# A head's outputs copied behind two exponentials of the next head, and added behind the second low part

## What is computed

```python
# attention: 32 query heads, 8 key/value heads of 64, rope, causal mask
attn = jnp.einsum('bkgqd,bkld->bkgql', qh, kh) * SCALE
attn = jnp.where(causal[None, None, None], attn, -jnp.inf)
p = jax.nn.softmax(attn, axis=-1)
out = jnp.einsum('bkgql,bkld->bkgqd', p, vh)
...
return out @ Wo.T
...
x = _layernorm(x + attn_ref(x, Wq, Wk, Wv, Wo))
x = _layernorm(x + xattn_ref(x, fside, ctx))      # two SmoothQuant int8 products with silu between
x = _layernorm(x + ffn_ref(x, up, down, scales))  # sign weights, relu, 512 -> 2048 -> 512
```

## Time and profile before

| | |
|---|---|
| median of 3 runs | 1396.93 us (1396.26 to 1397.88) |
| the profiled execution | 1396.48 us, its span 1394.7 us |
| PE busy (matmuls) | 1295.6 us, 93% of the span |
| DVE busy | 1011.3 us, 73% |
| ACT busy | 905.3 us, 65% |
| POOL busy | 782.9 us, 56% |
| granted TensorE clock | 0.98 of full speed |

### The profile page before, as it was taken

One profiled execution on the slowest core, in us unless ns is written; L12 is line 12 of the kernel. 1 busy time (PEld: TensorE's weight loads), 2 busy tenths in 40 slices (PEclk: granted clock), 3 DMA queues, 4 the chain that ended last, 5 costly groups with the idle time before them and its releaser, 6 DMA issues.

```text
span 1394.7 us, 25191 instructions
## 1 busy us (share of the span) xinstructions
PE 1295.6 (93%) x7112; PEld 1077.2 (77%) x7112; DVE 1011.3 (73%) x2492; ACT 905.3 (65%) x2140; POOL 782.9 (56%) x685
## 2 busy tenths in 40 slices
PE   5899999999999999899989998999987998999996
PEld 3788878888888877777878787878876775878784
DVE  3677777776777767888987888778886787965322
ACT  3676777777767776667776776777666764565332
POOL 4555565555655675646864556586651253746453
PEclk8999999999999999999999999999999998999998
DMA  4722222222222223333222222322224502100000
GB/s 138 231 62 54 63 59 65 62 69 63 72 60 54 61 54 92 91 91 84 66 65 72 57 66 50 91 58 69 63 57 133 213 16 76 47 16 31 1 31 30
DMA packets 55285, 98.78 MB, mean 71 GB/s; under 512 B 11792, under 2 KB 13840, under 8 KB 54288
## 3 DMA queue, kind: packets, MB, share of 16 engines
q1 hardware_dynamic: 55184, 97.57, 25.2%
HBM read 51.39 MB, written 4.19 MB: 40 GB/s over the span
## 4 chain that ended last, share of the span: by engine, by line
PE 76%; DVE 9%; ACT 6%; issue 5%; POOL 2%; SPq 0%; DMA 0%; ACTq 0%; DVEq 0%; POOLq 0%
PE m L1846 30%; PE ps_s L1846 9%; PE ps_o L1903 9%; PE m L2128 7%; PE ps_t L1891 7%; PE ps_s L2142 4%; PE ps_t L2142 3%; DVE pT_lo L1556 2%; PE m L1913 2%; ACT pT_hi L1271 2%; DVE o_sum L1499 1%; ACT probs L1263 1%; DVE probs L1485 1%; PE pc L2007 1%; POOL o_lo L1089 1%
## 5 line engine op out<-in xcount | busy, mean ns | idle before, releaser
L1263 ACT ACTIVATE probs<-probs,neg_max 128x128 f32<-128x128 f32 (+3 forms) x512 | 285.3, 559 | 156.2 <-DVE neg_max L1485 155.5
L1556 DVE TENSOR_TENSOR pT_lo<-ps_t,pT_hi 128x512 fp32r<-128x512 f32 (+1 forms) x384 | 221.0, 596 | 140.9 <-ACT pT_hi L1271 138.5
L1485 DVE CUSTOM_DVE_ANT_0 probs<-ps_s,mask 128x128 f32<-128x128 f32 (+3 forms) x512 | 228.4, 482 | 9.5 <-PE ps_s L1846 9.4
L1846 PE MATMUL ps_s<-k_st,q_st 128*128 128x256 f32 (+2 forms) x1024 | 231.8, 348 | 2.6 <-DMA q_st<-q_tmp 2.2
L1891 PE MATMUL ps_t<-ident,probs 128*128 128x128 f32 x1280 | 185.3, 276 | 45.6 <-DVE pT_lo L1556 35.5
L1891 PEld LDWEIGHTS ps_t<-ident,probs 128*128 128x128 f32 x1280 | 147.2, 141 | 70.5 <-DVE pT_lo L1556 44.9
L1271 ACT ACTIVATE pT_hi<-ps_t 128x512 fp32r<-128x512 f32 (+1 forms) x384 | 186.2, 520 | 13.3 <-PE ps_t L1891 10.3
L1089 POOL TENSOR_TENSOR o_lo<-o_sum,o_hi 128x512 fp32r<-128x512 f32 x64 | 82.0, 1281 | 193.8 <-ACT o_hi L1285 193.7
L1903 PE MATMUL ps_o<-pT_hi,v_st 128*128 128x256 f32 (+2 forms) x512 | 169.4, 342 | 0.0
L1139 POOL TENSOR_TENSOR hid_lo<-hid,hid_hi 128x512 fp32r<-128x512 f32 x64 | 83.1, 1299 | 133.5 <-ACT hid_hi L1450 133.4
L1903 PE MATMUL ps_o<-pT_lo,v_st 128*128 128x256 f32 (+2 forms) x512 | 156.3, 327 | 0.0
(11 more groups left out here) (259 smaller groups left out, 3068.8 us busy)
## 6 DMA issues: line engine op xcount, KB each, us to landing
q_st<-q_tmp SPq DMA_DIRECT2D x512, 64.0 KB, 2.0
raw<-in_wq_t SPq DMA_DIRECT2D x32, 256.0 KB, 3.0
k_st<-k_st SPq DMA_DIRECT2D x64, 128.0 KB, 2.3
raw<-in_wo_t SPq DMA_DIRECT2D x32, 256.0 KB, 2.9
raw_b<-in_ffn_t SPq DMA_DIRECT2D x10, 512.0 KB, 6.8
raw<-in_wkv_t SPq DMA_DIRECT2D x16, 256.0 KB, 3.5
y<-in_x SPq DMA_DIRECT2D x4, 1024.0 KB, 7.1
w_gu<-in_fside_t SPq DMA_DIRECT2D x4, 1024.0 KB, 7.1
```

The source lines that it names most:

```text
L1263: act.activation(probs[:, h % 2, SO[i]:SO[i] + SW[i]], probs[:, h % 2, SO[i]:SO[i] + SW[i]], ACT.Exp, bias=neg_max[:, h % 2, i:i + 1], sca ...
L1485: dve.tensor_tensor_reduce(out=probs[:, h % 2, SO[i]:SO[i] + SW[i]], in0=ps_s[:, i % 2, 0:SW[i]], in1=mask[:, L - SW[i]:L], scale=-SCALE, ...
L1556: dve.tensor_tensor(pT_lo[:, d, :], ps_t[:, (h + k) % 2, 0:P * w].rearrange("p (w c) -> p w c", c=P), f32(pT_hi[:, d, :]), ALU.subtract).t ...
L1846: i = pe.matmul(dst, a, c, start=(j == 0), stop=(j == len(terms) - 1))
```

## The change

Two calls move; nothing is added or taken away. On ACT `copy_o(n - 1)` moves from the start of head n to a place behind `high_p` 0 and 1 and the first two exponentials of head n+1, ahead of `high_p` 2. On DVE `add_o(n - 1)` moves from a place ahead of the low part of block 1 to a place behind it. `values`, and all else on PE, stay as they are.

```diff
@@ ACT, body
                     for h in range(G):
                         n = u * G + h
                         more = nxt or h < G - 1
-                        if prev or h > 0:
-                            copy_o(n - 1, (h - 1) % G)
                         high_p(n, h, 0)
                         high_p(n, h, 1)
                         for what in weights_in(g, b, h):
...
                         if more:
                             exp(n + 1, (h + 1) % 2, 0)
                             exp(n + 1, (h + 1) % 2, 1)
+                        if prev or h > 0:
+                            copy_o(n - 1, (h - 1) % G)
                         high_p(n, h, 2)
@@ DVE, body
                             if k == 0 and more:
                                 softmax_max(n + 1, (h + 1) % 2, 0)
                                 softmax_max(n + 1, (h + 1) % 2, 1)
-                            if k == 0 and (prev or h > 0):
+                            if k == 1 and (prev or h > 0):
                                 add_o(n - 1, (h - 1) % G, u * 2 + (h - 1) // 2)
```

## The result

The changed kernel takes 1436.35 us (median of 4 runs, 1435.17 to 1438.01), the kernel before 1396.95 (1396.26 to 1397.88). The ratio is 1.0293, with an interval from 1.0277 to 1.031: it is slower by about 41 us by that ratio (39.4 us by the two medians). The forecast was 1413.5 us with a range up to 1421. The direction was right; the loss is about 2.4 times as large as forecast (41 us against 17), and the time lies outside the range.

A forecast was written before the change was run, and what follows sets the result against it. It took PE, the fullest engine, to be held by waits for DVE's low parts and ACT's exponentials. Five loop steps gave 6.5 us, eleven others 1.0 each: +17.5, rounded to +17 on 1396.48, 1413.5 us; range 1402.5 to 1421.

The forecast's parts named there:

- two routes to PE: Lateness reaches PE directly through DVE's low part at (0, 1) and through POOL at (1, 1): 1413.5 us, chance 0.62.
- front wait: PE idle for the first low part at (1, 0) and (1, 1): shrinks from 0.76 to about 0.51 us, -0.25.
- back wait at (0, 1): (0, 2)'s first transpose waits for (0, 1)'s last exponential; DVE's lateness stretches (0, 1) by +0.69 us, +0.5 in the loop.
- POOL's route at (1, 1): k's late rounding delays POOL's four operations, then q's second rounding and the exponentials: (1, 1) +0.74 us.
- only the direct route: Rival: POOL's chain or the `recips` term does not bind; near +8, 1404.5 us, chance 0.24.
- `recips` term: At (0, 0), (0, 2) and (1, 2), DVE's later `add_y` delays `recips`: +0.1 us each, +0.3 a step.
- What hides the rest: At h = 3 and (1, 2) projections cover the exponentials; a short cover for q priced nothing to +0.5 us a unit.
- a new wait at h = 3: Sign that the prediction is wrong: new waits standing at the heads h = 3; no size given.
- `values` needs the addition only at the end of a head: Part of what hides the rest: PE's `values` needs DVE's addition only then; no cost in the sum.
- A late copy is partly hidden: In the eleven written-out steps, later parts' items partly hide the copy: two thirds taken, 1.0 us each, 11 in all.
- held operation: In three steps a small DVE operation ahead of (1, 1)'s first low part ends with POOL's run: up to +1.1 us each.

The follow-up runs named there:

- e5: Both moves (ACT's copy, DVE's addition) at head (1, 0) alone, against the kernel before: 1406.63 us, ratio 1.0078.
- e7: Both moves at heads (0, 0), (0, 2) and (1, 2) alone, those with `recips`, against the kernel before: 1409.48 us, ratio 1.0104.
- e11: Both moves at the two heads h = 3 only, against the kernel before: 1396.99 us, ratio 1.0013.
- e9: Both moves in the last eight of the sixteen steps only, against the kernel before: 1417.93 us, ratio 1.016.
- e6: Both moves at head (1, 1) alone, against the kernel before: 1399.19 us, ratio 1.0029.
- e10: Both moves at heads (1, 0) and (1, 1) together, against the kernel before: 1405.42 us, ratio 1.0079.
- e12: Only ACT's copy moved, behind the first block's rounding, at five heads a step; DVE's order as in the kernel before: 1389.27 us, ratio 0.9958.

## Why the prediction was right, and where it was wrong

The direction and the two routes to PE were right. The sum was wrong in two steps: the term for `recips` was too small, and the steps that are written out were discounted where they cost more than the loop's.

**The front wait (-0.25): right.** 0.76 became 0.51 us; (1, 0) measured -0.24 in the loop and -0.16 to -0.19 in most of the written-out steps.

**The back wait at (0, 1) (+0.69, in the loop +0.5): right.** +0.67 in step 6, +0.44 in the loop.

**POOL's route at (1, 1) (+0.74): right.** +0.73, with every station within 0.1 us, though the last 0.1 us is luck (see above), and e5 shows it by itself. The rival "only the direct route" (+0.2 there) falls.

**The `recips` term (+0.1 a head): mis-sized, and it is the largest part of the miss.** The step said that `add_y` would end at 6.65 "plus a signal", 0.08 us past the old start of `recips` at 6.57. At (1, 2) it ended at 6.73 (420.38 - 413.65), because DVE is 0.59 us late there and not 0.5, and `recips` started 0.13 us behind that (420.51). So `recips` came 0.29 us later in place of 0.1. In steps 6 and 8 each of the three heads lost 0.20 to 0.27 us, in the loop (0, 0) even 0.41. I had treated a difference between two numbers of 6 us as if each were exact to a few hundredths. An error of 0.1 us in each came on top of a result of 0.1. The room between the two was also read at one of the three heads only: before the change `add_y` ended 0.42 us ahead of `recips` at (1, 2) of a loop step, but 0.35 us ahead at (0, 0) and 0.15 at (0, 2). Over the 124 heads the three places measured +17.2 us against 3.7 in the sum: 13.5 of the 24 us that are missing. A part of the 13.5 is the discount of the late steps, and a part the clock; both follow below. e7, at these places alone, gives +14.5.

**"What hides the rest": nearly right.** e11 has +1.8 us; the bound set in the prediction, up to 0.5 us a unit, held it. The (0, 3) part is the early `out3`, which waits for DVE's `add_y` like `recips` does. The prediction had named a new wait at h = 3 as a sign of being wrong; this is one, and it is small. Its words that `values` needs the addition only at the end of a head failed in ten places (6.1 us of waits, above).

**"A late copy is partly hidden" (two thirds, 1.0 us a written-out step): wrong, and it has the wrong sign.** e9 has 2.8 us a late step. At a head where an item of the later parts fills DVE at the start, it hides not the cost but the gain. Head (0, 2) of step 14 after, DVE and then PE:

```profile
1009.01 0.68 DVE L1614 TENSOR_REDUCE sm_a<-xs 128x1 f32<-128x512 f32 x1
1009.60 0.68 DVE L1556 TENSOR_TENSOR pT_lo<-ps_t,pT_hi 128x512 fp32r<-128x512 f32 x1
...
1012.16 0.69 DVE L1493 TENSOR_TENSOR o_sum<-ps_o,o_part 64x512 f32<-64x512 f32 x1 [0.72 <-ACT o_part L1278]
...
1014.31 0.68 DVE L1508 TENSOR_TENSOR y<-y,m 128x512 f32<-128x512 f32 x1
```

```profile
1015.05 0.66 PE L1913 MATMUL m<-ident,r_rep 128*128 128x128 f32 x4 [0.60 <-DVE y L1508]
```

The head starts at 1007.64. Its first low part starts 1.96 us in, the same as before the change (975.17 - 973.21), since DVE is still busy with the later part's reduction. The earlier rounding on ACT is worth nothing there. The maxima and exponentials stay where they were, the copy ends at 4.49 (3.84 at the same place of step 6), and `add_y` ends 0.69 us later than before, where at the same place of step 6 it ends 0.33 later. PE waits 0.60 us, and the head loses 0.72 where the forecast's term gave 0.07. e9 shows the same at this head (+0.71).

**The held operation (up to +1.1, in the range only): right in size.** The head (1, 1) of step 8 starts at 606.33; DVE:

```profile
607.63 4.21 DVE L1636 TENSOR_SCALAR y<-y,mv_n,norm_n 128x512 f32<-128x512 f32 x1
611.77 0.68 DVE L1556 TENSOR_TENSOR pT_lo<-ps_t,pT_hi 128x512 fp32r<-128x512 f32 x1
```

POOL:

```profile
610.31 1.25 POOL L1056 TENSOR_TENSOR q_tmp<-q_tmp 128x512 f32<-128x512 f32 x1
```

It took 3.51 us before and takes 4.21 now, and again it ends 0.28 us behind POOL's run (611.84 and 611.56). PE waited 4.65 us for the low part where it had waited 3.60. In steps 10 and 12 the wait grew from 3.21 to 4.22 and from 3.72 to 4.78, so the three places gave 3.1 us of waits, which the sum left out and the range took in. The Trainium skill ("SBUF — State Buffer", Who interferes with whom) has the lock held for one instruction; by that the operation would have stayed short. Both rows speak against it. e5 and e6 bear on the cause. e5 leaves the orders at (1, 1) as they were and makes only POOL's run late: the operation takes 4.21 us and PE waits 4.66. e6 makes the change at (1, 1) and leaves POOL's run early: 3.54 and 3.62 us. So its length goes with the place of POOL's run. That POOL's instructions hold DVE back one after the other is still inferred from the ends that coincide; no run here took POOL's run away.

**TensorE's clock: not in the forecast.** Head (0, 2) of step 11, in the changed kernel and in e9, which runs the same orders in this step. PE waited 0.80 us ahead of it in both. PE's rows, first the changed kernel:

```profile
796.49 1.85 PE L1891 MATMUL ps_t<-ident,probs 128*128 128x128 f32 x8 [0.80 <-ACT probs L1263]
797.99 1.20 PE L1846 MATMUL ps_s<-k_st,q_st 128*128 128x256 f32 x4
```

then e9:

```profile
779.68 1.06 PE L1893 MATMUL ps_t<-ident,probs 128*128 128x128 f32 x8 [0.80 <-ACT probs L1263]
780.50 0.72 PE L1848 MATMUL ps_s<-k_st,q_st 128*128 128x256 f32 x4
```

and the two stretches by windows (busy time by engine, then the granted clock), the changed kernel and e9:

```profile
796.50:800.50 4.00, 4.00 (x17) 3.72 (x18) 2.77 (x8) 2.68 (x8) 1.37 (x2) 0.57 0.43 99
```

```profile
779.70:783.70 4.00, 4.00 (x25) 3.58 (x26) 2.73 (x9) 3.21 (x10) 1.36 (x2) 1.00 0.45 103
```

The granted clock was 0.57 in one and 1.00 in the other: the lower level, 1.2 GHz, for most of the stretch against 2.4 GHz throughout. The head is 10.43 us long against 9.49, so a fall costs about 0.9 us at this place. A fall also stands behind the wait of 2.11 us ahead of (1, 2) in step 7 (546.91; clock 0.57 in the 4 us behind it, 1.00 before the change, where the wait was 1.31). The clock also stands inside the late steps' figures. Head (1, 1) of step 8 by windows, in the kernel before, the changed kernel and e11:

```profile
589.06:600.01 10.95, 7.35 (x38) 5.83 (x37) 9.06 (x18) 6.21 (x17) 6.73 (x7) 0.84 0.23 51
606.33:619.77 13.44, 8.79 (x38) 7.04 (x37) 10.72 (x18) 6.71 (x18) 8.01 (x7) 0.75 0.21 46
591.47:603.82 12.35, 8.73 (x38) 6.99 (x37) 9.54 (x18) 6.20 (x17) 7.20 (x7) 0.72 0.26 58
```

The head grew by 2.48 us and PE's wait in it by 1.05. The other 1.4 us are the clock: e11 changes nothing here, PE waits 3.62 us as before, and at a granted clock of 0.72 the head is 1.40 us longer all the same. e10 has the same head with the changed kernel's wait (4.65 us) and a granted clock of 0.86, near that of the kernel before, and there it is only 1.07 us longer. In step 10 it goes the other way: the wait grew by 1.01 us and the head by 0.06. On one chip the fifteen executions of the kernel before go from 1393.31 us at a mean clock of 0.984 to 1397.55 at 0.980.

How much of the whole it is can be bounded for the two profiled executions: span times (1 - mean clock) is 27.9 us before (clock 0.980) and 31.6 after (0.978), so about 4 us of the 41, give or take 1.4 for the rounding of the two clocks. Why it fell in the one execution and not in the other is open.

What stays open in the late steps: the four explanations (lost gain, held operation, direct waits for `add_y` in the last step, clock) are each read from single heads and were not undone one by one, and what share of the late steps each has is not shown. e9 shows only their sum, +22.3 us for eight steps.

## What to carry to other kernels

When an instruction is moved from a place where it costs part of its length into a busy stretch, it costs its full length there, and what waits for it on the other engine can add to that (at (0, 1) 0.48 us of lateness from the copy and 0.2 from the addition, after the 0.25 us that were won); ask what follows it there up to the bounding engine, and through a third engine too. A small result that is the difference of two long sums (here 6.65 against 6.57) deserves a range of the size of the errors in those sums, and counts as often as the place repeats: 47 heads, priced 0.29 us too low on average, made more than half of the miss. Steps with extra work on the waiting engine are not discounted by a fraction: look at one of them, since extra work can hide the gain and leave the cost; and try the smallest move that takes the wait away (e12) before the largest. A trace of one execution holds waits and clock falls that another does not; compare single heads only where several runs agree on them.

## What the runs showed of the hardware that was not expected

A signal costs more at some places of the loop than in the steps that are written out. From the end of ACT's copy to the start of DVE's waiting addition are 0.13 us at (0, 0) and (1, 0) in the loop's steps, and 0.03 us at every other place where it waits, at the same two heads of the written-out steps too. From the end of `add_y` to PE's matmul of `recips` at (0, 0) are 0.17 to 0.18 us in the five loop steps and 0.06 in the ten steps behind them; at (0, 2) and (1, 2) of the loop it is 0.13. One of the loop's is

```profile
370.60 0.68 DVE L1508 TENSOR_TENSOR y<-y,m 128x512 f32<-128x512 f32 x1
```

```profile
371.46 0.65 PE L1913 MATMUL m<-ident,r_rep 128*128 128x128 f32 x4 [0.21 <-DVE y L1508]
```

(371.28 to 371.46). The second of these signals makes up about half of the difference at (0, 0), which lost 0.41 us in the loop and 0.20 in step 6; the rest is mostly that `add_y` ended 0.35 us ahead of `recips` there before the change, and 0.43 us ahead in step 6. What in the loop makes the signals longer was not tested.
